# Order of the work on VectorE, ScalarE, GpSimd and the queue in groups 0, 1, 15, 16, 23, 24 and the tail, and the place of group 0's first product

## The reference

```python
attn = jax.nn.softmax(jnp.einsum('btd,bTd->btT', x @ Wq, x @ Wk) * scale, axis=-1)
attn_out = jnp.einsum('btT,bTd->btd', attn, x @ Wv) @ Wp + bp
cms_out = jax.nn.gelu(attn_out @ cW1 + cb1, approximate=False) @ cW2 + cb2 + target_embed
concat = jnp.concatenate([attn_out, cms_out], axis=-1)
modifier = jax.nn.gelu(concat @ mW1 + mb1, approximate=False) @ mW2 + mb2
x = jnp.clip(x + cms_out + modifier, 0.0, 1.0)
h = jax.nn.gelu(x @ W_down[stream] + b_down[stream], approximate=False) @ W_up[stream] + b_up[stream]
h = layer_norm(x + h) * ln_w[stream] + ln_b[stream]
```

## Time and profile before

| | |
|---|---|
| median of 3 runs | 1111.81 us (1111.11 to 1112.79) |
| profiled execution | 1112.28 us |
| its span, first to last instruction | 1110.5 us |
| mean granted TensorE clock | 0.991 |
| TensorE busy | 1071.2 us (96%), 4736 matmuls |
| VectorE, ScalarE, GpSimd busy | 593.6, 454.8, 538.1 us |
| DMA | 100.51 MB, mean 91 GB/s |

### The profile page before, as it was taken

How to read it: one execution, slowest core, us unless ns; L and a number is a source line. 1 busy time by engine, 2 the same in 40 slices (tenths; PEclk the granted TensorE clock), 3 DMA queues, 4 the chain that set the end, 5 groups by cost and what they waited for, 6 DMA issues and landing times.

```text
span 1110.5 us, 13134 instructions
## 1 busy us (share of the span) xinstructions
PE 1071.2 (96%) x4736; PEld 882.9 (80%) x4736; DVE 593.6 (53%) x837; ACT 454.8 (41%) x871; POOL 538.1 (48%) x555
## 2 busy tenths in 40 slices
PE   7999999999999999999979999999699999999996
PEld 6888888778888888888768888888478888888885
DVE  3634343485555555655835445454665445444667
ACT  3524335353352343244444433334443333443664
POOL 0501154442242142143777666776776677663415
PEclk9999999999999999999989999999899999999999
DMA  7301010101114122111302222226634221224753
GB/s 266 130 5 38 1 38 20 39 0 44 71 72 142 71 82 95 45 51 39 127 30 90 72 81 81 73 71 230 239 121 164 81 70 54 67 67 149 278 113 115
DMA packets 62064, 100.51 MB, mean 91 GB/s; under 512 B 5680, under 2 KB 35376, under 8 KB 61488
## 3 DMA queue, kind: packets, MB, share of 16 engines
q1 hardware_dynamic: 61424, 98.62, 26.1%
q10 hardware_dynamic: 576, 1.05, 0.2%
HBM read 77.63 MB, written 22.02 MB: 90 GB/s over the span
## 4 chain that ended last, share of the span: by engine, by line
PE 87%; DVE 6%; POOL 2%; ACT 2%; DMA 1%; issue 1%; SPq 0%; DVEq 0%; ACTq 0%; POOLq 0%
PE bank L732 29%; PE bank L733 29%; PE bank L734 29%; DVE z L1473 1%; DMA c_B_f<-cms_kept 1%; DVE stats L1467 1%; DVE c_T_f L1284 1%; POOL W_lo L565 1%; PE bank L776 1%; POOL left_x L565 1%; DVE c_T_lo L1307 0%; ACT acc L1082 0%; DMA WqT_raw<-WqT_dram 0%; DVE H_lo L1334 0%; DVE acc L1363 0%
## 5 line engine op out<-in xcount | busy, mean ns | idle before, releaser
L565 POOL TENSOR_TENSOR left_x<-rawX,left_x 128x256 fp32r<-128x256 f32 x144 | 126.5, 879 | 175.0 <-ACT left_x L962 175.0
L732 PE MATMUL bank<-H_hi,W_hi 128*128 128x512 f32 x512 | 200.6, 392 | 7.3 <-POOL W_lo L565 7.0
L1363 DVE TENSOR_TENSOR acc<-bank,acc 128x512 f32<-128x512 f32 x224 | 152.1, 688 | 97.8 <-PE bank L734 97.5
L733 PE MATMUL bank<-H_lo,W_hi 128*128 128x512 f32 x512 | 200.3, 391 | 0.0
L734 PE MATMUL bank<-H_hi,W_lo 128*128 128x512 f32 x512 | 200.1, 391 | 0.0
L962 ACT ACTIVATE left_x<-rawX 128x256 fp32r<-128x256 f32 x144 | 57.9, 410 | 167.6 <-DMA rawX<-mW_dram 87.4
L732 PEld LDWEIGHTS bank<-H_hi,W_hi 128*128 128x128 f32 x512 | 96.8, 189 | 28.4 <-POOL W_lo L565 7.4
L1346 DVE TENSOR_TENSOR u_t<-bank,s_t 128x512 f32<-128x512 f32 x64 | 44.2, 691 | 133.4 <-PE bank L734 129.6
L733 PEld LDWEIGHTS bank<-H_lo,W_hi 128*128 128x128 f32 x512 | 96.8, 189 | 20.2
L734 PEld LDWEIGHTS bank<-H_hi,W_lo 128*128 128x128 f32 x512 | 96.8, 189 | 20.1
L732 PE MATMUL bank<-x_T_hi,left_x 128*128 128x512 f32 x256 | 100.4, 392 | 9.2 <-DVE u_t L1346 4.6
(11 more groups left out here) (187 smaller groups left out, 2298.2 us busy)
## 6 DMA issues: line engine op xcount, KB each, us to landing
rawX<-mW_dram SPq DMA_DIRECT2D x16, 512.0 KB, 3.5
rawC<-mW_dram SPq DMA_DIRECT2D x16, 512.0 KB, 5.5
W_raw<-mW_dram SPq DMA_DIRECT2D x16, 512.0 KB, 3.7
xT_raw<-xT_dram SPq DMA_DIRECT2D x4, 1024.0 KB, 8.2
x_raw<-x_dram SPq DMA_DIRECT2D x4, 1024.0 KB, 5.9
rawX<-cW_dram SPq DMA_DIRECT2D x8, 512.0 KB, 3.7
W_raw<-cW_dram SPq DMA_DIRECT2D x8, 512.0 KB, 3.7
out_dram<-z SPq DMA_DIRECT2D x16, 256.0 KB, 2.0
```

The costliest lines, as they stand in the source:

```text
L565: pool.tensor_tensor(dst, src, f32(hi), ALU.subtract).then_inc(done, 1)
L732: pe.matmul(tile, sh, mh, start=first_one and n == 0, stop=False, skip_group_check=joined_group)
L733: pe.matmul(tile, sh, ml, start=False, stop=False, skip_group_check=joined_group)
L1363: op = dve.tensor_tensor(dst, src, dst, ALU.add)
```

## The change

No operation is added and none removed; instructions move on each engine's list, with the counts of the waits that depend on it.

- TensorE: product 0 of g0 stands ahead of the last four attention tiles.
- g0 and g1: VectorE makes the sum T3 (x operands, second pair) and T1's low part in g1, between the C21 and the C12 low parts, and T3's low part before the evictions; ScalarE makes the high parts of T3 and T4 behind `keep_first(1)`.
- g15: VectorE's sum T2 (cms) stands behind JC21.
- g16: on VectorE, U2 stands behind the first of four low parts, B22's behind U3. GpSimd and ScalarE take the cms left parts 5 and 6 earlier, W2 earlier on both, and the two next sets in a mixed order.
- g23: SP's queue brings both cms blocks ahead of the x1 blocks. VectorE makes the sums T1, T2, T4 behind C11's low part, T3 in g24. ScalarE and GpSimd split W2 before the C21 GELU and before left part 5.
- g24: T3, B21, T4, B22 high parts around `keep_first`; T1's and T3's low parts before the evictions; T4's low part on GpSimd, from g23, between B21's and B22's.
- Tail: `add_b_up(2)` before `y_final(3)`, `add_b_up(3)` behind the first four norms, `gelu_lo_adapter(3)` ahead of `layer_norm(1)`.

The lists of three places, first before, then after. VectorE in g16: the low parts of the first pair's cms operands, then the joins U2 (`u2_t<-bank1`), U3 (`u3_t<-bank1`) and JC22.

```diff
-        CO_HI_ORDER = [(B11, B21, T1, T2, T4, T3, B22), (B11, T2, T3, T4, T1, B21, B22)]
+        CO_HI_ORDER = [(B11, B21, T1, T2, T4, T3, B22), (B11, T2, T1, T3, B21, T4, B22)]
...
                 if g == 23:
                     sp.wait_ge(made, products(g, 0))
                     cms_home(0, B11, B21)
-                    x1_home(0)
                     sp.wait_ge(made, products(g, 1))
                     cms_home(1, T3, B22)
-                    for i in range(1, 5):
+                    for i in range(5):
                         x1_home(i)
...
                 if q == 1:
-                    pool.wait_ge(co_step[1], 1 if op == B11 else 4)
+                    pool.wait_ge(co_step[1], {B11: 1, B21: 3, T4: 3, B22: 4}[op])
...
                     left_lo(1, 0, 4)
                     left_lo(*sets[0], 0)
-                    sum_2(*sets[0])
-                    left_lo(*sets[0], 1)
                     for i in (5, 6):
                         left_lo(1, 0, i)
+                    sum_2(*sets[0])
+                    for i in (1, 2):
+                        left_lo(*sets[0], i)
                     second_lo(second_set(g))
-                    for i in (2, 3):
-                        left_lo(*sets[0], i)
-                    sum_4(*sets[0])
-                    left_lo(*sets[0], 4)
                     sums_13(*sets[1])
                     left_lo(*sets[1], 0)
                     sum_2(*sets[1])
-                    for i in (1, 2, 3):
+                    left_lo(*sets[0], 3)
+                    left_lo(*sets[1], 1)
+                    sum_4(*sets[0])
+                    left_lo(*sets[0], 4)
+                    for i in (2, 3):
                         left_lo(*sets[1], i)
                     sum_4(*sets[1])
                     left_lo(*sets[1], 4)
...
                     if g == 24:
-                        for op in (B21, B22):
+                        for op in (B21, T4, B22):
                             co_lo(1, op)
...
                     for s, t in sets:
                         left_lo(s, t, 4)
+                if g == 23:
+                    second_lo(second_set(g))
                 for s, t in sets:
                     left_lo(s, t, 5)
                 if g in PIECE_GROUPS:
                     piece_split(g - 3)
-                if g == 23:
-                    co_lo(1, T4)
...
-                if g > MOD0:
+                if g > MOD0 and g != 23:
                     second_lo(second_set(g))
...
-            pe.wait_ge(lo_made, LAST)
-            for m in range(KT):
-                attn_tile(LAST + m, m)
...
+            pe.wait_ge(lo_made, pos[B - 1, "A", 0] + 1)
+            product_part(0, 0, [0])
+            pe.wait_ge(lo_made, LAST)
+            for m in range(KT):
+                attn_tile(LAST + m, m)
...
-                for i in order_of(g)[:2]:
+                for i in order_of(g)[g == 0:2]:
                     product_part(g, i, sources)
...
                     if op in (T1, T2, T3, T4):
-                        act.wait_ge(co_step[1], (T1, T2, T3, T4).index(op) + 1)
+                        act.wait_ge(co_step[1], (T1, T2, T4, T3).index(op) + 1)
...
                 if g == 24:
-                    for op in (B21, B22):
+                    co_hi(1, T3)
+                keep_first(g)
+                if g == 24:
+                    for op in (B21, T4, B22):
                         co_hi(1, op)
-                keep_first(g)
                 if g == 0:
                     xo_hi(1, T2)
+                if g == 1:
+                    for op in (T3, T4):
+                        xo_hi(1, op)
                 for i in (0, 1):
                     for s, t in sets:
                         left_hi(s, t, i, g)
+                    if g == MOD0 and i == 0:
+                        act.wait_ge(cms_saved[1], 16 * KT)
+                        for k in (5, 6):
+                            left_hi(1, 0, k)
...
-                if g == MOD0:
-                    act.wait_ge(cms_saved[1], 16 * KT)
-                    for i in (5, 6):
-                        left_hi(1, 0, i)
                 for s, t in sets:
                     left_hi(s, t, 2, g)
+                if g == MOD0:
+                    second_hi(second_set(g))
+                gelu(g, C11)
+                if g == MOD0:
+                    left_hi(*splits_in(g)[1], 0, g)
                 if g == 23:
                     co_hi(1, B11)
-                gelu(g, C11)
-                if g == MOD0:
-                    second_hi(second_set(g))
                 if last:
                     y01_to_hi(0)
                     y01_to_hi(1)
                 for s, t in sets:
                     left_hi(s, t, 3, g)
+                if g == MOD0:
+                    left_hi(*splits_in(g)[1], 1, g)
+                for s, t in sets:
+                    left_hi(s, t, 4, g)
+                gelu(g, C22)
+                if g == MOD0:
+                    left_hi(*splits_in(g)[1], 2, g)
                 if g == 23:
                     co_hi(1, T2)
-                for s, t in sets:
-                    left_hi(s, t, 4, g)
-                if g == 23:
-                    co_hi(1, T3)
-                gelu(g, C22)
+                    second_hi(second_set(g))
+                gelu(g, C21)
                 if g == MOD0:
-                    left_hi(*splits_in(g)[1], 0, g)
-                gelu(g, C21)
-                if g == 0:
-                    xo_hi(1, T3)
-                    xo_hi(1, T4)
-                if g == MOD0:
-                    for i in (1, 2, 3, 4):
+                    for i in (3, 4):
                         left_hi(*splits_in(g)[1], i, g)
                     sets = splits_in(g)
                 for s, t in sets:
                     left_hi(s, t, 5, g)
                 if g == 23:
-                    co_hi(1, T4)
                     co_hi(1, T1)
                 if g in PIECE_GROUPS:
                     piece_to_hi(g - 3)
-                if g > MOD0:
+                if g > MOD0 and g != 23:
                     second_hi(second_set(g))
...
             gelu_adapter(1)
+            add_b_up(2)
             y_final(3)
             gelu_adapter(2)
-            add_b_up(2)
-            add_b_up(3)
             for t in range(TT):
                 norm(t)
+            add_b_up(3)
             gelu_adapter(3)
...
                 if g > 0:
                     gelu_low(g - 1, C21)
+                if g == 1:
+                    minus(xo[1][T3], parts(xo[1], B22), parts(xo[1], T3), xo_step[1])
+                    xo_lo(T1)
+                if g > 0:
                     gelu_low(g - 1, C12)
+                if g == 24:
+                    co_sum(1, T3)
                 if g == MOD0:
                     co_sum(0, T4)
                     add_outputs(g - 1, 0)
                     co_sum(0, T3)
                     co_lo(0, T2)
                     add_outputs(g - 1, 1)
-                    for op in (T1, T3, T4, B22):
+                    co_lo(0, T1)
+                    join(g, U2)
+                    for op in (T3, T4):
                         co_lo(0, op)
-                    join(g, U2)
...
                     else:
                         if g == 1:
-                            xo_lo(T1)
                             dve.wait_ge(xo_step[1], 2)
                             xo_lo(B21)
+                            xo_lo(T3)
+                        if g == 24:
+                            for op in (T1, T3):
+                                co_lo(1, op)
                         add_outputs(g - 1, 0)
-                    if g == 24:
-                        for op in (T1, T3):
-                            co_lo(1, op)
                     if g == 1:
-                        for op in (T3, T4):
-                            xo_lo(op)
+                        xo_lo(T4)
                         dve.wait_ge(xo_step[1], 3)
                         xo_lo(B22)
...
-                if g == 23:
-                    co_sum(1, T1)
-                    co_sum(1, T2)
                 join(g, U3)
+                if g == MOD0:
+                    co_lo(0, B22)
                 join(g, JC22)
                 if g == 0:
                     xo_lo(T2)
                 else:
                     gelu_low(g, C11)
                 if g == 23:
-                    co_sum(1, T3)
-                    co_sum(1, T4)
-                    co_lo(1, T2)
+                    for op in (T1, T2, T4):
+                        co_sum(1, op)
                 if g > 0 and g != MOD0:
                     add_outputs(g - 1, 1)
                 if g == 24:
                     clip(1, outputs(g - 1, 1, KT - 1))
                 if g == MOD0 - 1:
                     co_sum(0, T1)
+                join(g, JC21)
+                if g == MOD0 - 1:
                     co_sum(0, T2)
-                join(g, JC21)
                 if g == 0:
                     gelu_low(g, C11)
+                if g == 23:
+                    co_lo(1, T2)
```

(4 more changed lines are left out.)

## The result

The changed kernel takes 1091.68 us (median of 4 runs, 1091.46 to 1092.58) against 1112.3 us (4 runs, 1111.11 to 1112.86). The ratio is 0.9822, with a 95% interval of 0.981 to 0.9834: 20.6 us less, where 21.8 were forecast (from three of these four runs, with a median of 1111.81 us). The profiled execution took 1091.48 us (span 1089.7), so 20.8 us less than the profiled one of before.

The account below looks back on a forecast made before the run. TensorE, busy 1071.2 us of a 1110.5 us span, was taken as the bound, so only its holes and the end could give time: 3.8 + 9.4 + 5.0 + 3.6 = 21.8 us, forecast 1090.0 us, range 1086 to 1093.5.

Parts of the forecast that it names:

- the main case: Whole kernel: the four stretches gain 21.8 us, giving 1090.0 us, own range 1086 to 1093.5, chance 0.58.
- Groups 0 and 1: g0 and g1: moved product and reordered low parts remove the 2.40 us hole; 3.8 us gained.
- Groups 15 and 16: g15 and g16: earlier joins and weights start g16's output tiles sooner; 9.4 us gained, ends 7.5 and 11.3.
- The left part B11: g16, next cms set: ready at 565.6, wanted by TensorE at 565.3, against a 4.14 us hole before.
- rival 2: g16: left part B11 misses TensorE, a 4.14 us hole and slow matmuls stay; 5.8 us less, 1095.8 us, chance 0.16.
- Groups 23 and 24: g23 and g24: 12.0 us won in g23, part given back in g24; 5.0 us kept, ends 3.0 and 12.0.
- The mis-sized term: g24, VectorE after C11's GELU at 816.1: four evictions (2.5 us), clipping of the second half and JC21, at about 821.5.
- The signs: New profile, g24: the largest middle hole, 3 to 5 us, stands before the output tiles, released by W_lo.
- Rival 1: g24: no give-back, GpSimd's operations beside VectorE being as short as alone; 28.8 us gained, 1083.0 us, chance 0.20.
- rival 4: Whole kernel: the moves don't act, waits being set by transfers or TensorE itself; 1111.8 us, chance 0.02.
- Rival 3: g23: each us W lands after 788.1 costs TensorE one; loss from 30.5 us landing, 40 us gives 1121.5; chance 0.02.
- The tail: End of kernel: moved additions and low parts start the last tile at 1101.2, not 1104.84; 3.6 us gained, at most 4.0.

Follow-up runs that it names:

- e7: Changed kernel with g0's first product put back behind the last four attention tiles: 1093.53 us.
- the second profile: The changed kernel run and profiled once more, with no edit: 1092.35 us.
- e4: Changed kernel with ScalarE's and GpSimd's order in g16 put back to that of before, VectorE's new order kept: 1095.71 us.
- e6: Changed kernel with VectorE's order in g16 put back (U2 behind all four low parts), ScalarE's and GpSimd's new order kept: 1095.21 us.
- e3: Changed kernel with T4's high part (ScalarE) and low part (GpSimd) in g23 ahead of W's parts, the low part not in g24: 1091.22 us.
- e5: Changed kernel with C11's GELU in g24 ahead of the high parts of the next sets' left part T2 on ScalarE: 1091.65 us.
- e9: e5 with W's parts also ahead of C21's GELU and of left part 5 in g24: 1092.31 us.
- e10: e9 plus x1 blocks 3 and 4 behind W in g23, T4's parts in g23 (low part behind W_lo), last two x1 blocks behind next raw blocks: 1089.99 us.
- e11: e10 plus earlier raw-block requests in g24, VectorE's low part T2 ahead of JC21 in g23, GpSimd's low part T4 heading its g24 row: 1088.46 us.
- e2: Changed kernel with one more x1 block (number 5, 1 MB) ahead of W in SyncE's queue in g23: 1094.35 us.

## Why the prediction was right, point by point

1091.68 us lies in the main case's own range, 1086 to 1093.5. Times of the first profile are put on the old clock by what TensorE had gained before: 4.13 us in g16, 13.67 in g23 and g24.

**Groups 0 and 1** went as counted: the T3 product at 217.76 (forecast 218.06), output tiles at 226.07 (226.22) and 235.59 (235.75), no hole in g1. e7 confirms that the product's move keeps only part of its length.

**Groups 15 and 16.** JC21 and JC12 gave 0.16 us, not 0.35. In g16 the count went through an engine chain of ten steps and ended at 571.7; measured 571.0 in the first profile and, with the usual collision, 572.1 in the second. The left part B11 was forecast 0.3 us late; the first profile has no hole there, the second one of 0.24 us. e4 and e6 show the two halves as they were argued: rival 2, a 4.14 us hole that stays, is just what e4 brings back when ScalarE's and GpSimd's order is undone. The near hit of 9.70 for 9.4 is in part luck: with the usual collision the stretch gives 8.6 us.

**Groups 23 and 24** have the step that failed. The first part held: W lands at 787.8 (forecast 788.1), output tiles of g23 at 791.94 (792.2), the cms half of T1 at 799.70 (799.5), so 11.8 us had been won there. C11's GELU of g24 ends at 816.1, as counted. The mis-sized term is what VectorE does from there to JC21: counted 5.4 us, to 821.5, measured 6.7, to 822.8. Rows of VectorE, ScalarE and GpSimd:

```profile
801.73 0.68 ACT L1054 ACTIVATE gelu_f<-bank,bias 128x512 f32<-128x512 f32 x1
...
802.44 1.04 DVE L1340 TENSOR_TENSOR H_lo<-gelu_f,H_hi 128x512 fp32r<-128x512 f32 x1 [4.29 <-ACT gelu_f L1054]
803.40 2.47 DVE L1369 TENSOR_TENSOR acc<-bank,acc 128x512 f32<-128x512 f32 x4
805.91 2.62 DVE L1386 TENSOR_SCALAR acc<-acc 128x512 f32<-128x512 f32 x4
808.45 0.68 DVE L1352 TENSOR_TENSOR s_t<-bank,s_t 128x512 f32<-128x512 f32 x1
...
810.88 0.93 POOL L564 TENSOR_TENSOR left_x<-rawX,left_x 128x256 fp32r<-128x256 f32 x1 [2.97 <-ACT left_x L964]
...
813.16 2.35 POOL L564 TENSOR_TENSOR W_lo<-W_raw,W_hi 128x1024 fp32r<-128x1024 f32 x1
```

The clips took 2.62 us beside GpSimd (four take 1.43 us at 1044.02, where GpSimd rests), and C11's low part 1.04. The output tiles of g24 started at 829.24, just past the 828.1 to 829 that were named, and the sum had used the early end; with 1.76 us of slow clock (1.65 forecast) 3.7 us are kept, not 5.0. Also missed: JC21 frees the bank of g25's T2 product, so the hole came in two parts, 2.48 and 1.77 us, each with slow matmuls behind it; those behind the first lie in what would else be wait for W_lo (3.36 us in the second profile, which has none there). The signs named one hole of 3 to 5 us, though the sum's own terms, 828.1 less 822.7, give 5.4. Rival 1 (no give-back, 1083.0) and rival 4 (the moves don't act) are refuted; e3, e5 and e9 show that GpSimd's row is its cause, and e10 and e11 that the queue's order is the next bound. Rival 3's price, one us of TensorE for each us of W, is what e2 measured (2.40 us for 2.5), and its place is real: ScalarE waited 5.99 us for W at 774.10. Its example with 40 us comes to 1121.3 us by its own sum, not 1121.5.

**The tail**: last stats at 1084.00, which is 1101.39 on the old clock (forecast 1101.2), 3.4 us for 3.6.

## What to carry to other kernels

Follow each gained hole until the chains that do not move with TensorE have caught up: the queue's own waits and one full engine row gave back 1.3 us more than counted here, and up to 6.5 us in the runs that went further. Of a transfer that sits behind others in a queue, ask when it is asked for and what is ahead; moving its wait on an in-order engine is only as good as its landing. Count VectorE and GpSimd as taking turns where VectorE's instruction has both its inputs in SBUF, and give a chain of ten such steps a spread of 1 us.
